# Ten block ends of a graph network layer pair: one meeting of the engines in place of two, and no wait of POOL for its queue

## What is computed

```
xn = _layernorm(x)
x = x + _L0_gnn_ref(xn, ...) + _L0_mix_ref(xn, ...)      # typed graph attention, 8 types, 8 heads; linear attention
x = x + _L0_ffn_ref(_layernorm(x), ...)                  # shared MLP and 2 of 8 experts for each node
xn = _layernorm(x)
x = x + _L1_gnn_ref(xn, ...) + _L1_mix_ref(xn, ...)      # graph convolution, then one-head graph attention; linear attention and MLP
x = x + _L1_ffn_ref(_layernorm(x), ...)                  # MLP on the upper half of the nodes
```

## Time and profile before

| | |
|---|---|
| time, median of three runs | 2839.17 us (2838.43 to 2846.54) |
| time of the profiled execution | 2842.59 us |
| its span, first to last instruction | 2840.8 us |
| busy share of the span | PE 81%, POOL 48%, DVE 46%, ACT 38% |
| mean granted clock of TensorE | 0.891 of full speed |
| instructions recorded | 42657 |

### The profile page before, as it was taken

One profiled execution on the slowest core, in us unless ns is written; L12 is line 12 of the kernel. 1 busy time (PEld: TensorE's weight loads), 2 busy tenths in 40 slices (PEclk: granted clock), 3 DMA queues, 4 the chain that ended last, 5 costly groups with the idle time before them and its releaser, 6 DMA issues. The chain is left out here.

```text
span 2840.8 us, 42657 instructions
## 1 busy us (share of the span) xinstructions
PE 2288.4 (81%) x11329; PEld 1709.0 (60%) x11329; DVE 1314.0 (46%) x3509; ACT 1076.3 (38%) x2885; POOL 1376.8 (48%) x1407
## 2 busy tenths in 40 slices
PE   6899847767777988999997797777754798886898
PEld 5454534445455876888886465455544676764577
DVE  6553456766676130111113332343239666666851
ACT  3333544544441212233333443255420655553211
POOL 0221477777730051122221577777767777776300
PEclk9999867888788899999998898988775899999899
DMA  3476644444411024777774433344547444443300
GB/s 98 157 217 221 182 110 122 119 120 119 120 53 36 16 90 145 204 223 195 210 216 138 139 106 106 105 128 124 158 111 254 137 132 150 132 130 97 108 14 32
DMA packets 249527, 374.45 MB, mean 132 GB/s; under 512 B 66472, under 2 KB 186740, under 8 KB 249322
## 3 DMA queue, kind: packets, MB, share of 16 engines
q0 software_dynamic: 70000, 179.80, 22.9%
q1 hardware_dynamic: 132740, 140.88, 16.3%
q10 hardware_dynamic: 46582, 51.38, 5.4%
HBM read 298.68 MB, written 73.27 MB: 131 GB/s over the span
## 5 line engine op out<-in xcount | busy, mean ns | idle before, releaser
L2794 POOL DMA_INDIRECT cm_rows<-rows,e_bsrc x392 | 373.0, 952 | 175.5 <-issue 96.9
L1182 POOL DMA_INDIRECT store<-rows,e_bsrc x392 | 378.6, 966 | 119.4 <-issue 109.0
L1529 POOL DMA_INDIRECT at_rows<-values,e_brow x362 | 344.3, 951 | 115.1 <-issue 89.3
L1609 PE MATMUL at_part<-at_msg,store 128*128 128x265 f32 x880 | 269.7, 449 | 86.1 <-DVE at_msg L1765 42.2
L2931 PE MATMUL cm_part<-cm_rows,cm_one 128*128 x880 | 264.7, 443 | 88.9 <-SPq L2807 58.9
L1209 PE MATMUL banks<-ag_msg,ag_one 128*128 128x258 f32 x880 | 227.3, 396 | 67.8 <-issue 44.7
L2931 PEld LDWEIGHTS cm_part<-cm_rows,cm_one 128*128 128x128 f32 x880 | 179.8, 218 | 157.5 <-issue 134.2
L1609 PEld LDWEIGHTS at_part<-at_msg,store 128*128 128x128 f32 x880 | 175.8, 218 | 156.6 <-DVE at_msg L1765 65.5
L2231 POOL DMA_INDIRECT x_sum<-x_y,x_target x56 | 87.1, 1555 | 340.7 <-DVE x_y L2344 333.4
L3147 DVE TENSOR_TENSOR store<-store,cm_part 128x256 f32 x220 | 92.2, 419 | 339.7 <-PE cm_part L2931 311.7
L1209 PEld LDWEIGHTS banks<-ag_msg,ag_one 128*128 128x128 f32 x880 | 164.5, 194 | 114.9 <-issue 56.3
(11 more groups left out here) (700 smaller groups left out, 3923.7 us busy)
## 6 DMA issues: line engine op xcount, KB each, us to landing
x_w<-in_L_ffn_W1p SPq DMA_DIRECT2D x32, 1024.0 KB, 5.2
x_w<-in_L_ffn_W2p SPq DMA_DIRECT2D x32, 1024.0 KB, 5.5
values<-at_rows ACTq DMA_DIRECT2D x25, 1088.0 KB, 5.9
p_brow<-local_row SPq DMA_DIRECT2D x44, 320.0 KB, 4.1
xn_acc<-low_row SPq DMA_DIRECT2D x28, 448.0 KB
expert_in<-store POOLq DMA_DIRECT2D x7, 1040.0 KB, 8.3
at_rows<-values,e_brow POOLq DMA_INDIRECT x392, 2.8
cm_rows<-rows,e_bsrc POOLq DMA_INDIRECT x392, 2.7
```

The source lines that it names most:

```text
L1182: pool.indirect_dma_start(rows[:, b % slots, k, :], None, table, bass.IndirectOffsetOnAxis(index[:, k, b:b + 1], 0)).then_inc(gathered[b % ...
L1529: pool.indirect_dma_start(rows[:, b % RING, k, :], None, table, bass.IndirectOffsetOnAxis(e.block_row[:, k, b:b + 1], 0)).then_inc(gathere ...
L1609: last = pe.matmul(part[:, bank["pair", n], 0:wide], one[:, n // U % 2, k, n % U, :], msg[:, n % 4, k, :], start=(k == 0), stop=(k == K2 - 1))
L2794: pool.indirect_dma_start(rows[:, b % SLOTS, k, :], None, table, bass.IndirectOffsetOnAxis(e.block_src[:, k, b:b + 1], 0)).then_inc(gather ...
```

## The change

A block is opened with `no_gpsimd_drain=True`. Its closing meeting is then of another form: SP, ACT, DVE and PE each run a DRAIN and after it a semaphore instruction of its own that tells POOL; POOL runs no DRAIN, only the wait for the four and the release. The second meeting is gone at nine of the ten ends. The clear stays on POOL, behind the release, and still has its own DRAIN (with the range of numbers that it resets) ahead of each EVENT_SEMAPHORE_RANGE_CLEAR. Since the other engines may by then be in the next block, `signal` gives that block only numbers that the last clear does not touch. The numbers of a block are therefore no longer always one range: POOL clears two ranges at ends 3 and 8 and three at end 4, fourteen in all where it cleared ten. At end 8 (`apart=True`) a second meeting stays, in a form without DRAINs. No instruction of PE, DVE, ACT or POOL that computes, and no DMA, is added, left out or moved.

```diff
 TOGETHER = []
+CLEARED = set()
+
+
+def signal(nc, name):
+
+    free = [n for n in nc.free_semaphores if n not in CLEARED]
+    return nc.alloc_semaphore(name, min(free))
+
+
+def retire(nc, sems):
+
+    CLEARED.clear()
+    CLEARED.update(s.num for s in sems)
+    nc.clear_and_free_semaphores(sems)
 
 
 @contextmanager
-def together(nc):
+def together(nc, apart=False):
     with ExitStack() as memories:
         sems = []
-        with nc.Block() as block:
+        with nc.Block(no_gpsimd_drain=True) as block:
             TOGETHER.append((block, sems, memories))
             yield
             TOGETHER.pop()
-        nc.clear_and_free_semaphores(sems)
-        nc.all_engine_barrier()
+        retire(nc, sems)
+        if apart:
+            nc.all_engine_barrier(sem_only=True)
+            CLEARED.clear()
 
 
 @contextmanager
 def stage(nc, *names, ended=()):
     here = next(STAGES)
-    sems = [nc.alloc_semaphore(f"{n}_{here}") for n in names]
+    sems = [signal(nc, f"{n}_{here}") for n in names]
     if TOGETHER:
         TOGETHER[-1][1].extend(sems)
         yield (TOGETHER[-1][0], *sems)
         return
-    with nc.Block() as block:
+    with nc.Block(no_gpsimd_drain=True) as block:
         yield (block, *sems)
-    nc.clear_and_free_semaphores([*sems, *ended])
-    nc.all_engine_barrier()
+    retire(nc, [*sems, *ended])
...
-                gathered = [nc.alloc_semaphore(f"gathered{b}") for b in range(RING)]
+                gathered = [signal(nc, f"gathered{b}") for b in range(RING)]
...
-                    with together(nc):
+                    with together(nc, apart=True):
                         folded = fold_scores(nc, w2e, a["L1_gnn_W2"], a["L1_gnn_att_src"], a["L1_gnn_att_dst"], (wqt, g))
```

## The result

The changed kernel takes 2820.18 us (median of 4 runs, 2812.42 to 2824.17); the kernel before, on the same chip, 2842.35 us (median of 4, 2838.43 to 2846.54). The ratio is 0.992 with a 95% interval of 0.9903 to 0.9937, a gain of 18 to 28 us; the medians are 22.2 us apart, against a sum of 21.2 us. The forecast of 2818 us started from a median of 2839.17 us for the kernel before; from 2842.35 the same sum would have given 2821.2.

What follows compares the result with a forecast made beforehand. PE was taken to bound the experts' and final blocks, POOL's gathers the convolution and both attentions. 4.2 + 4.63 + 5.19 + 3.34 + 3.8 = 21.2 us off 2842.59, with the median 3.4 us lower, gave 2818 us; range 2813 to 2831.

Steps and rivals of the forecast that it cites:

- Rival C: At the block ends: the next block's code may load during the meeting, so 4.2 us are lost; 2822 us; chance 6%.
- rival B: At the clears: their DRAIN inherits the removed POOL DRAIN's wait, leaving a gain of 9.6 us; 2829.5 us; chance 15%.
- E: Other stretches, such as loads issued sooner beside transfers under way, swallow part of the gain; up to 2829.5 us; chance 7%.
- Second meeting: All ten ends: dropping or trimming the second meeting saves 4.2 us, net of 0.4 us for added semaphore instructions.
- End 6: First meeting: POOL comes at 1529.5 in place of 1534.15; 4.63 us, all of it for SP, ACT and DVE.
- End 8: First meeting: POOL comes at 2109.6 in place of 2114.8; 5.19 us, if the clear's DRAIN does not wait.
- End 9: The others are let go when DVE ends its DRAIN, not POOL; 3.34 us, with POOL ready in time for DVE.
- End 3: Ahead of the first attention: POOL's first gather comes at 354.2 in place of 358.01; 3.8 us, bounds 0.2 and 4.8.
- paced by gathers, whatever the other engines do: Both attentions and the convolution end later or sooner with POOL's first gather; 1.256 to 1.271 us per gather.
- The clear's DRAIN, taken as short: At each clear: POOL's DRAIN stays as short as before, 88 to 213 ns, rather than taking the removed one's length.
- it waits for something of POOL's queue: End 6, first meeting: POOL's 4.631 us DRAIN waits for something in its queue, neither its compute nor its transfers.
- Rival D: PE-paced blocks: shorter PE idle could lower the granted TensorE clock; 5% less costs 30 us, 2848 us; chance 4%.

## Why the prediction was right, point by point

- **The whole**: 2818 us forecast, 2820.18 measured, within 2813 to 2831; the 22.2 us between the medians stand against the 21.2 of the sum, and the gain's interval is 18 to 28 us. The forecast's chances don't add up as told: forecast, C and two thirds of B alone make 0.84, with most of E some 0.89.
- **Second meeting, 4.2 us**: in the traces 4.5 us, with the DRAIN kept. As time it is not shown by itself: the run that takes it alone has an interval with nothing in it too. Rival C (the second meeting's time isn't given back), 4 us off the forecast, falls by the traces only: at end 6 SP issues 0.1 us behind the release, at end 9 DVE idles 0.41 us.
- **End 6, 4.63 us**: ACT, which starts the block with SP, idled 14.38 us ahead of it and now 9.20, 5.18 us less; 4.63 + 0.55 (the second meeting) is 5.18.
- **End 8, 5.19 us**: POOL's pause fell from 8.35 to 3.14, 5.21 us, and the two releases are 0.95 us apart (1.0 forecast).
- **End 9, 3.34 us**: DVE's idle fell by 4.37 us, against 3.34 + 1.11 = 4.45 with the second meeting, and POOL was not late.
- **End 3, 3.8 us**: POOL's pause fell by 3.87 us. The step "paced by gathers, whatever the other engines do" holds for a late POOL, 10.7 us held and 11.3 us late at the last gather. It is too strong for the others: they may be late by 4 us at most, by the block's end perhaps by none. Here both were let go sooner, so the term stood.
- **The clear's DRAIN, taken as short**: 67 to about 200 ns at 13 of 14, so rival B falls. The mark "under 0.3 us at end 3" was set wrong: it took 2.18 us there, and all but 0.1 us of it was gathers still to be issued. The pause behind them (1.23 us, 1.3 forecast) counts the clear fully, in bounds of 0.2 to 4.8 us of gain.
- **Where the reasoning was wrong without cost**: "it waits for something of POOL's queue". At the four ends it was not waiting. It took its own time, 0.082 us for each DMA up to about 100 of them, and so it costs the same whenever it runs. The size of each term was right because it was read from the trace before, not because the cause was known: no rule here gives the lengths at ends 8 and 9. Rival B's 9.6 us rested on a wait that time would cover, and at end 9 that was wrong by 6.6 us: 1.7 us of gain in its sum, 4.9 of loss in the run with the DRAIN at the clear.
- **Rival D (clock)**: the granted clock is 0.900 over the span, 0.891 before, so it falls.

The sentence of the Trainium skill (PSUM — Partial Sum Buffer, "Engine vs sequencer instructions") that a drain waits for the engine to go fully idle fits the clear's DRAIN (it ends 0.1 us behind the last gather off the engine) and is not the whole of the plain one (5.11 us behind an engine that was idle for 44.5 us).

## What to carry to other kernels

Look for a long DRAIN of an engine that issues many DMAs, and compare its start with the end of that engine's last work: what lies behind is a price that no earlier finish and, here, no later place made cheaper, so take it out or put it where nobody waits for the engine. Price each block end twice, for the engine whose idle starts the next block's chain and for the one that paces it, and take a ring's slots as slack with a size, to be measured, not as a cover. A change worth 4 us of 2840 has to be read in the trace's idle times, since a dozen runs do not show it in the time.

## What the runs showed of the hardware

- POOL's plain DRAIN takes 0.0815 us for each DMA that POOL has issued since its last one, 20 to 100 of them, all landed, behind an idle engine (1.686 to 8.204 us). Over 100 it is not in proportion: 5.11 us for 362, 5.19 for 415, 9.19 for 394. With no plain DRAIN ahead, 511 DMAs took 4.638 us, what 56 take. Where DMAs are under way it also waits: three DRAINs ended 0.3 to 0.7 us behind the last landing, a fourth 0.14.
- The DRAIN in front of a semaphore clear is another kind: 67 to about 200 ns with 362 DMAs issued and no plain DRAIN in between, and where gathers are pending it ends 0.11 us behind the last one off the engine, 1.9 us ahead of its landing.
- A second meeting of five engines with a clear in it costs 0.52 to 1.11 us from release to release before, 0.90 of it at end 8; there it is 0.95 us now, without the four engines' DRAINs but with two clears in it, so the meeting without the clear is the smaller part.
